# Wide attention layer: the weighted values of a head pair over all four key tiles in one piece

## The reference

```
h = _modulate(_layernorm(x), sh_msa, sc_msa)
qkv = h @ W_qkv                                  # 256 -> 3 x 1024
attn = softmax(einsum('bqhd,bkhd->bhqk', q, k) * 64 ** -0.5)
out = einsum('bhqk,bkhd->bqhd', attn, v).reshape(B, T, 1024)
x = x + g_msa * (out @ W_out + b_out)
x = x + g_mlp * _ff(...)                         # gelu MLP, 256 -> 1024 -> 256
```

## Time and profile before

| | |
|---|---|
| median of three runs | 5845.14 us |
| profiled execution | 5844.69 us |
| its span | 5842.8 us |
| TensorE matmul busy, whole span | 5511.4 us (94%) |
| VectorE, ScalarE, GpSimd busy | 74%, 70%, 48% |
| the wide layer in the trace | 803 to 2223 us |

### The profile page before, as it was taken

The page is one execution under the profiler, slowest core; times in us unless marked ns, Lnnn a source line. Parts: engine busy times, 40 slices in busy tenths (PEclk is TensorE's granted clock), DMA queues, the critical chain, the costliest instruction groups (busy, mean ns, idle before and its releaser), DMA issues. The chain is left out here.

```text
span 5842.8 us, 74727 instructions
## 1 busy us (share of the span) xinstructions
PE 5511.4 (94%) x27336; PEld 2865.9 (49%) x27336; DVE 4311.1 (74%) x5020; ACT 4113.3 (70%) x6785; POOL 2804.3 (48%) x2191
## 2 busy tenths in 40 slices
PE   8999999999999997999998999999999999999998
PEld 5444445555555554444444444444544445454445
DVE  6767744444444444776867989899898999989898
ACT  3555454554444543555558989899998989989897
POOL 0000012232222321010106969699696978969697
PEclk8999999999999998999999999999999999999999
DMA  5342420000000004233223020110202012020200
GB/s 145 47 66 34 83 30 3 1 3 3 2 3 1 3 2 63 48 62 63 48 45 69 30 54 30 42 43 24 59 30 54 30 29 56 26 58 30 54 30 22
DMA packets 171934, 222.33 MB, mean 38 GB/s; under 512 B 40881, under 2 KB 107274, under 8 KB 171314
## 3 DMA queue, kind: packets, MB, share of 16 engines
q1 hardware_dynamic: 171570, 217.56, 17.1%
HBM read 152.90 MB, written 30.49 MB: 31 GB/s over the span
## 5 line engine op out<-in xcount | busy, mean ns | idle before, releaser
L2480 DVE TENSOR_TENSOR_SCAN l__h<-l__decay,psum 128x1024 f32<-128x1024 f32 x1024 | 2249.6, 2267 | 55.9 <-ACT l__decay L1928 15.5
L2446 POOL TENSOR_TENSOR l__hc<-l__h,l__c_rep 128x1024 f32<-128x1024 f32 x1016 | 2012.4, 2013 | 92.5 <-DMA l__c_rep<-l__c_dram 46.5
L1928 ACT ACTIVATE l__decay<-l__dt_rep,l__a_neg 128x511 f32<-128x511 f32 x2048 | 1339.6, 708 | 9.6 <-DVE l__h L2480 9.3
L1938 PEld LDWEIGHTS psum<-ident,l__dtx_B 128*128 128x128 f32 x8192 | 882.7, 141 | 850.9 <-DVE l__h L2480 496.1
L2564 PE MATMUL psum<-l__hc,l__gather 128*64 128x512 f32 x4096 | 1105.2, 618 | 139.8 <-POOL l__hc L2446 139.3
L1938 PE MATMUL psum<-ident,l__dtx_B 128*128 128x128 f32 x8192 | 1119.3, 280 | 35.6 <-DVE l__h L2480 16.8
L1912 ACT ACTIVATE l__dtx_B<-l__dtx_T,l__b_T 128x512 f32<-128x512 f32 x1664 | 1103.4, 709 | 5.5 <-PE psum L1938 3.4
L683 DVE TENSOR_REDUCE l__row_max<-psum 128x1 f32<-128x512 f32 x1024 | 648.7, 680 | 207.4 <-PE psum L717 203.8
L1367 POOL TENSOR_SCALAR l__probs<-l__probs,l__rec 128x512 f32<-128x512 f32 x512 | 348.6, 694 | 886.4 <-DVE l__rec L1363 886.4
L199 POOL TENSOR_SCALAR l__ln_var_eps<-l__ln_mean_var 128x4 f32<-128x4 f32 x56 | 16.1, 287 | 1433.6 <-DVE l__ln_mean_var L185 1433.6
L1040 ACT ACTIVATE l__probs<-psum 128x1024 f32<-128x1024 f32 x512 | 501.9, 1023 | 147.5 <-PE psum L1101 141.2
(11 more groups left out here) (184 smaller groups left out, 6193.9 us busy)
## 6 DMA issues: line engine op xcount, KB each, us to landing
l__c_rep<-l__c_dram SPq DMA_DIRECT2D x512, 128.0 KB, 2.8
l__dt_rep<-l__dt SPq DMA_DIRECT2D x128, 256.0 KB, 5.0
l__parts_dram<-l__parts SPq DMA_DIRECT2D x64, 384.0 KB, 3.5
l__q_stack<-l__parts_dram SPq DMA_DIRECT2D x192, 128.0 KB, 6.5
l__k_stack<-l__parts_dram SPq DMA_DIRECT2D x192, 128.0 KB, 9.1
l__w<-in_l_w SPq DMA_DIRECT2D x6, 1024.0 KB, 6.3
l__gate_rows<-l__gates_dram SPq DMA_DIRECT2D x24, 256.0 KB, 3.2
in_mod_w<-in_mod_w SPq DMA_DIRECT2D x1, 4608.0 KB, 17.8
```

Source lines behind the costliest of these rows:

```text
L1928: nc.scalar.activation(decay[:, i % DECAYS, s, 1:T], dt_rep[:, w, c, s, 1:T], ACT.Exp, scale=a_neg[:, g, c, s:s + 1]).then_inc(S["decay"], 1)
L1938: last = nc.tensor.transpose(bx_psum(i)[:, s, t * P:(t + 1) * P], dtx_B[:, (k + 1) % 2, t, 2 * c + s, :, :].rearrange("p j d -> p (j d)"), ...
L2446: nc.gpsimd.tensor_tensor(hc[:, i % HCS, :, :], h[:, i % HS, :, :], c_of(i), ALU.mult).then_inc(S["hc"], 1)
L2480: nc.vector.tensor_tensor_scan(both(h[:, i % HS, :, :]), both(decay[:, i % DECAYS, :, :]), both(bx_psum(i)), 0.0, ALU.mult, ALU.add).then_ ...
```

## The change

It takes `values` out of its two places in the rounds and puts all four key tiles at the end of the first round of each pair, for all pairs from 1 to 7. Nothing else of any engine's program differs.

```diff
                         transposes(n, j)
                     if projecting and n % TT < 3:
                         project_ahead(n)
-                    elif pair and not projecting:
-                        values(pair - 1, n % TT)
-                if pair and projecting:
-                    for n in both:
-                        values(pair - 1, n % TT)
+                if pair and u % TT == 0:
+                    for k in range(TT):
+                        values(pair - 1, k)
                 for n in both:
                     rows_ahead(n)
```

## The result

The changed kernel takes 5903.25 us (median of four runs, 5897.71 to 5914.07) beside 5846.55 us for the kernel before in the same series: 1.0099 times, 95% interval 1.0084 to 1.0114, or 49 to 67 us slower. The second series gave 1.0101 (1.0088 to 1.0115). Forecast were 5895 us and 5880 to 5906. The profiled execution took 5905.77 us, span 5903.9, 61.1 more than before.

What follows compares the result with a forecast made beforehand. TensorE's instructions plus its waits were taken to bound the wide layer. Per batch 2.84 + 3.73 = 6.57 us, 46.0 in seven, plus 4.1 in the last, gave +50 on 5845: 5895 us, range 5880 to 5906.

Steps and rivals of the forecast that it cites:

- the first part: Wide layer: it lasts as long as TensorE's instructions plus waits, so unchanged instructions leave mainly the waits to act.
- Part 1: Values in pairs 1 to 7: merging into 16 records saves 0.14 us per pair in 1 to 5, 0.46 in 6 and 7.
- Rival A: Fewer mode passages decide and the waits find slack: faster, 13 us in all, 5832 us; chance 0.03.
- Part 2: Passages out of pairs 1 to 4: second scores wait for ScalarE's last exponentials, costing 0.85; +0.71 us per pair, +2.84 together.
- Part 3: Pairs 5 to 7, with waits for VectorE's copies: 1.72 + 2.57 - 1.16 + 0.60 = +3.73 us.
- The clock: Granted clock after the new wait of about 2.1 us in pair 6: expected to hold, costed at nothing.
- Rival D: Clock falls to 1.2 GHz after pair 6's wait, slowing the values: 3.58 us in seven batches, 5920 us; chance 0.06.
- The sum: Whole kernel: 6.57 us a batch, 46.0 in seven, 4.1 in the last; +50 us, 5895 us.
- Rivals B and C: No change, within 5845 +- 8, chance 0.03; and pairs 5 to 7 coming out even, 5868 us, chance 0.08.

Runs made afterwards that it cites:

- the halves: Kernel before with the single piece only in pairs 1 to 5: 5885.3 us, 1.0062 times; only in pairs 6 and 7: 5862.2 us, 1.0023 times.
- the altered turns: Kernel before with v copied after the exponentials, ScalarE's second modulation later and VectorE's rows normalised in turn 24: 5834.5 us, 0.9978 times.

## Why the prediction was right, and where it was off

- **Which side and how much.** The time is in the range and the forecast's +50 us is at the lower edge of the measured 49 to 67. The loss is in TensorE's waits in the wide layer, as the first part said, and in its clock, which it costed at nothing.
- **Part 1**, the piece: 3.58 us and 0.14 gained per pair of the first kind; right, and borne out alone (0.47 left for three pairs, 0.42 expected). Rival A, that the fewer entries decide, is refuted in the placement chosen and true only where nothing is uncovered.
- **Part 2**, the passage: 2.77 us and +0.70 a pair against +0.71. The size was right because the row of pair 0 was the same order of instructions. The words on it were less so: I wrote that ScalarE's turns follow the transposes and yet weighed the wait by how late ScalarE's turn comes; it is a round trip that begins with TensorE itself. That error cost nothing in the prediction and 23 us in an expectation.
- **Part 3**, pairs 5 to 7: second round of pair 6, 5.28 us against 5.42; pair 7, 12.54 against 12.61; second transposes of unit 25 at 6.92 us after the first scores against 6.90 laid out. Clean batch +6.21 against +6.57, seven of them 43.5 against 46.0. Last batch +6.2 us to the end of its output projection, of which 2.9 are two falls, so +3.3 against 4.1. The waits for ScalarE's copy of head 0's transposes were not foreseen: I named waits of half a microsecond to one for VectorE's copy in units 27, 29 and 31, and in unit 27 it is 0.34 us for ScalarE's copy and then 0.29 for VectorE's. The transposes still start where they were laid out, 4.28 us into the round. The lower bound given for these pairs, -0.92, leaves out pair 5's own 0.14; nothing came near it.
- **The clock** is the mis-sized term: "I cost it at nothing". In the profiled execution the seven steps are 56.19 us longer in all, so the falls take 56.19 - 43.5 = 12.7 us of them, and 2.9 in the last batch, together 15.6. Rival D had the mechanism, with a chance of 0.06 and a price of 3.58 us in seven batches; it cost 1.70 us at unit 25 in five, and I had not seen the place in pair 7. The argument against it was one wait of 2.24 us at full clock, a single case: the same wait, in the same surroundings, is followed by a fall in two of the five traces that have it. What decides in which batches the clock falls is open.
- **The sum** closes: 43.5 + 12.7 + 6.2 = 62.4 us at the end of the wide layer, and the layers after it give 1.4 back, to 61.1. Part of the hit is luck: the falls alone, 15.6 us, are more than the 11 us between the forecast and the upper end of the range, and the time stayed inside because the laying out was 3.3 us too high (46.8 against 50.1) and the later layers gave the 1.4. One of the four runs, 5914.07, lies outside. Rivals B and C are out: the halves cost 4.53 and 1.68 us a batch.

## What to carry to other kernels

Work of the busiest engine that stands between two steps of a loop through other engines is the cover of that round trip: before moving it, measure the round trip from the producer's start to the consumer's start (2.63 us here) against what is left between them. Merging pieces pays by the entries saved (0.14 us here) and loses by the cover (0.85), so merge towards the uncovered place, not away from it. A wait of about two microseconds on TensorE can carry a second price in its clock (1.0 to 1.7 us here), paid in some repetitions and not in others; one undisturbed row is no proof that it is free.

## What the runs showed of the hardware

- The granted clock of TensorE fell to 0.51 of full in some of the batches of one execution and not in others, after waits alike to 0.03 us (2.06 to 2.09): 5 of 7, 4 of 7 and 3 of 7 in three profiles (the changed kernel twice, and with v's copy late). A fall cost 1.0 to 1.7 us.
- In the last batch a wait of 2.24 us, with a key tile of values on either side, had a fall after it in two traces (the single pieces at the end of odd pairs, alone and with the later modulation) and none in three (the kernel before, only pairs 1 to 5, the altered turns).
- Putting 1.72 us of useless matmuls into a wait of 2.08 us took that wait's falls away. Waits of 1.46 us in unit 25 (only pairs 1 to 5 changed) and 1.06 (only pairs 6 and 7) had none in seven batches each. The 1.70 us wait in pair 7 had none in the kernel before, with values between the transposes ahead of it, and a fall in two or three batches of seven in each of the six traces of versions where they were gone and the wait was left.
